# First self attention: who writes the high part of the queries, GpSimd or ScalarE

## The chip, the cores and the metric

The kernel runs on one core of a Trainium2 chip. The metric is the device time of one execution in microseconds (us); the times given are the median and the spread of several runs. A profile is one execution recorded by the hardware.

## The reference

A decoder of two layers runs over 8 sequences of 256 positions and 256 channels: attention, cross attention and a feed forward part, twice. Only the first attention matters here. It has 4 branches of 16 heads of 16 channels; all branches share keys and values. Cut to its core:

```python
q = (X @ W_Q + b_Q).reshape(Bv, Tv, H_TOT, DH).transpose(0, 2, 1, 3)
q, k = (_rope(q), _rope(k))
scores = jnp.einsum('bhtd,bhsd->bhts', q, k) * ATTNSCALE
w = jax.nn.softplus(scores / jnp.sqrt(key_self)[:, :, None, :])
w = jnp.where(causal, w, 0.0)
w = w * jax.nn.sigmoid(SCALE * w)
w = jnp.where(w < sinks, 0.0, w)
total = jnp.sum(w, axis=-1, keepdims=True) + sinks + 1e-06
out = jnp.einsum('bhts,bhsd->bhtd', w / total, v) + (sinks / total) * v_null
y = jnp.einsum('bntc,ncd->bntd', context, W_O) + W_O_bias[None, :, None, :]
```

`_rope` multiplies by a cosine and adds the other half of each pair times a sine.

## The kernel before

`attention0` writes out the order of every engine by hand. One pass of `over_batches` is a batch (a sequence) b, from -1 to 8: the work of batch b stands beside work ahead for b+1 and left over from b-1. A batch has 8 steps, one for each pair of heads; two steps are a quad of four heads. The first batch is b = 0, the second b = 1; "step 0" is the first step of a batch.

Scores: TensorE makes the scores of the next step in three slots (L386, L391), each as soon as ScalarE's softplus (L538) has emptied the slot's banks. ScalarE works slot by slot: step s, slots 0, 1, 2. In an even step it does more after slot 0: it copies the sums of an older quad out of PSUM (L525), then takes four silus (L557) over the quad before, with a table load on either side, then goes on with slot 1. In step 4 it also takes Ln and Exp for the keys (L564, L566) and copies the turned context (L515). VectorE compares each weight with its sink (L732, 16 instructions in an even step, two for each head and half) and so releases TensorE's weighted sums (L412). Between them VectorE takes other results out of two spare PSUM banks that everything else on TensorE shares in turn: the rotated queries and keys (L683), values (L691), regrouped sums (L703), the output (L722).

Queries are made a quad at a time, in even steps: the third quad of the batch in step 0, the fourth in step 2, and the first and second quad of the next batch in steps 4 and 6. Their path: TensorE projects (L435), VectorE multiplies by sine and cosine into `by_sin` and `by_cos` (L683), SP swaps neighbouring rows of `by_sin` into `turned_sin` by two DMAs (L332), GpSimd adds (`split_queries`) and splits the sum into a high part, rounded to the fp32r type, and the rest: `q_parts`. SP stores both (L337), waits, and loads them into rows (L341), all in the order of one queue, with the keys' store and loads (L349, L353) behind those of steps 4 and 6. Keys go the same way in step 2 (`square_keys`, L599 and L602) and step 4 (`split_keys`, L607 to L613). GpSimd also divides the sums of a quad (`divide`, L625 and L632). SP, GpSimd, ScalarE, VectorE and TensorE each run their own list in order and wait on semaphores. VectorE writes new rotations only when `rot_taken` says that the one before is used up.

In `split_queries` GpSimd waits for the swap, and for the rows of the previous quad to have landed (`q_here`), and then runs three 128x512 instructions: the sum into the high part (L590), the same sum into `by_cos` in full precision (L591), and the difference (L593).

Of the kernel before, what the change touches and what calls it, by code (L numbers as in the profile page):

```python
# [11 lines left out]
ALU = mybir.AluOpType  # L12
ACT = mybir.ActivationFunctionType
# [32 lines left out]
class Steps:  # L46
# [10 lines left out]
    def wait(self):  # L57

        self.eng.wait_ge(self.sem, self.base + self.n)
# [9 lines left out]
def alone(eng, sem, value, passed):  # L69

    eng.wait_ge(sem, value)
    eng.sem_inc(passed, 1)
# [22 lines left out]
def wait_alone(eng, sem, value, passed):  # L95
    if not isinstance(value, int) or value > 0:
        alone(eng, sem, value, passed)


def over_batches(eng, body):  # L100

    for b in range(-1, B + 1):
        body(b, 0 <= b < B, b + 1 < B, b >= 1)
# [97 lines left out]
PAIRS_OF_HEADS, QUADS, SLOTS = NH // 2, NH // 4, 3  # L201
# [30 lines left out]
def spare_bank(b, step, kind, i):  # L232

    return 6 + (SPARE_USES[step, (kind, i)] + b * len(SPARE_USES)) % 2
# [11 lines left out]
def quad_at(b, at, new, old):  # L246

    if at >= 0:
        return (at, b * QUADS + at) if new else None
    return (QUADS + at, b * QUADS + at) if old else None  # L250


def attention0(nc, norm, x_all, xnT_all, ident, psum, a):
    with ExitStack() as stack:
        s = Scope(nc, stack, "a0")
# [15 lines left out]
        by_cos, by_sin, turned_sin = (s.sb(n, [P, 2, T]) for n in ("by_cos", "by_sin", "turned_sin"))  # L271
        q_parts = s.sb("q_parts", [P, 2, 2, T], F32R)
# [23 lines left out]
        swapped, rot_taken, q_summed, q_split = (s.sem(n) for n in ("swapped", "rot_taken", "q_summed", "q_split"))  # L296
        ksq_ready, ln_k, knorm_ready, knormed, k_high, k_split = (
            s.sem(n) for n in ("ksq_ready", "ln_k", "knorm_ready", "knormed", "k_high", "k_split"))
        q_here, k_here = s.sems("q_here", 2), s.sems("k_here", 2)
        q_stored, k_stored = s.sem("q_stored"), s.sem("k_stored")  # L300

        scored, plus_done, silu_done, weights_done, summed, sums_taken = (
            s.sem(n) for n in ("scored", "plus_done", "silu_done", "weights_done", "summed", "sums_taken"))
# [5 lines left out]
        consts, passed, own = s.sem("consts"), s.sem("passed"), s.sem("own_setup")  # L309
# [11 lines left out]
        MOVES = 16 * PARTS  # L321
# [180 lines left out]
        @block.scalar  # L502
        def _(act):
            act.preload_act_table_set("softplus")
            act.wait_ge(consts, 1)

            def body(b, new, ahead, old):
                exists = {HERE: new, AHEAD: ahead, OLD: old}

                def take_turned(i):  # L510
                    spare = psum[:, spare_bank(b, 3 + i // 2, "turn", i), :]
                    act.wait_ge(turn_done, (b - 1) * 4 + i + 1)

                    wait(act, out_done, (b - 1) * TT + i // 2)
                    act.activation(ctxT[:, 4 * (i % 2):4 * (i % 2) + 4, :],  # L515
                                   spare.rearrange("p (k n) -> p k n", k=4), ACT.Copy).then_inc(turn_taken, 1)

                def take_sums(quad, half, bank):
                    if quad:
                        k, n = quad  # L520
                        act.wait_ge(summed, 2 * n + half + 1)
                        if half == 0:

                            wait(act, regrouped, (n - 1) * 2)
                        act.activation(sumT[:, k % 2, half * 512:(half + 1) * 512], psum[:, bank, :],  # L525
                                       ACT.Copy).then_inc(sums_taken, 1)

                def softplus(step, x):
                    pair = b * PAIRS_OF_HEADS + step
                    n = pair * SLOTS + x  # L530
                    if x == 0:

                        wait(act, summed, ((pair - PAIR_RING) // 2 + 1) * 2)
                    act.wait_ge(scored, n + 1)
                    wu = w[:, pair % PAIR_RING]
                    to, of = (wu[:, :, 2 * x:2 * x + 2, 0:T], psS[x].rearrange("p (h r t) -> p h r t", h=2, r=2)) if x < 2 else \
                        (wu[:, :, :, T:COLS], psS[x].rearrange("p (h r t) -> p h r t", h=2, r=BR))
                    act.activation(to, of, ACT.Softplus).then_inc(plus_done, 1)  # L538

                for step in range(PAIRS_OF_HEADS):  # L540
                    for x in range(SLOTS):
                        if new:
                            softplus(step, x)
                        if step % 2 == 0 and x == 0:
                            sums_quad = quad_at(b, step // 2 - 2, new, old)
                            take_sums(sums_quad, 0, spare_bank(b - (step < 1), (step - 1) % PAIRS_OF_HEADS, "sum", 0))
                            if old and step == 4:
                                take_turned(0)
                                take_turned(1)
                            quad = quad_at(b, step // 2 - 1, new, old)  # L550
                            if quad:
                                k, n = quad
                                act.wait_ge(plus_done, (n * 2 + 2) * SLOTS)
                                for pair in range(2):
                                    for h in range(2):
                                        wu = w[:, (2 * n + pair) % PAIR_RING, h].rearrange("p r t -> p (r t)")
                                        act.activation(wu, wu, ACT.Silu, scale=SILU_SCALE).then_inc(silu_done, 1)  # L557
                                        if (pair, h) == (0, 1):
                                            take_sums(sums_quad, 1, spare_bank(b, step, "sum", 1))
                            if ahead and step == 4:  # L560

                                act.preload_act_table_set("natural_log_exp_and_others")
                                act.wait_ge(norm_taken, b + 2)
                                act.activation(ksq[:], ksq[:], ACT.Ln).then_inc(ln_k, 1)  # L564
                                act.wait_ge(ln_k, b + 2)
                                act.activation(ksq[:], ksq[:], ACT.Exp, scale=-0.5, bias=ln_quarter[:, 0:1])\  # L566
                                   .then_inc(knorm_ready, 1)
                            if quad or ahead and step == 4:
                                act.preload_act_table_set("softplus")
                            if not quad:  # L570
                                take_sums(sums_quad, 1, spare_bank(b, step, "sum", 1))
                        if old and (step, x) == (5, 0):
                            take_turned(2)
                            take_turned(3)

            over_batches(act, body)

        @block.gpsimd
        def _(pool):
            pool.wait_ge(consts, 1)  # L580

            def body(b, new, ahead, old):
                exists = {HERE: new, AHEAD: ahead, OLD: old}

                def split_queries(n, r):

                    alone(pool, swapped, 32 * (r + 1), passed)

                    wait_alone(pool, q_here[(n - 1) % 2], (n - 1) // 2 * MOVES + MOVES if n > 0 else 0, passed)
                    pool.tensor_tensor(q_parts[:, 0], by_cos[:], turned_sin[:], ALU.add)  # L590
                    pool.tensor_tensor(by_cos[:], by_cos[:], turned_sin[:], ALU.add).then_inc(q_summed, 1)  # L591
                    alone(pool, q_summed, n + 1, passed)
                    pool.tensor_tensor(q_parts[:, 1], by_cos[:], q_parts[:, 0].bitcast(F32), ALU.subtract).then_inc(q_split, 1)  # L593
                    alone(pool, q_split, n + 1, rot_taken)

# [1573 lines left out]
def experts(nc, norm, x_all, xnT_all, ident, psum, a):  # L2169

    with ExitStack() as stack:
# [125 lines left out]
        def _(dve):  # L2297
# [75 lines left out]


STAGES = (("a0", attention0), ("x0", linear_attention), ("f0", switch_attention),
          ("a1", attention1), ("x1", cross_attention1), ("f1", experts))

# [120 lines left out]
```

## Time and profile before

| | |
|---|---|
| median of 3 runs | 2862.13 us (2858.52 to 2868.64) |
| the profiled execution | 2852.82 us, its span 2851.0 us |
| mean granted TensorE clock | 0.935 of full speed |
| the first attention in the span | about 28 to 720 us |
| batch b = 3 in the span | about 306 to 387 us |

The profile's busy time counts the work of an engine and not its waiting. A row of a timeline merges neighbouring instructions of one kind: start, length from the first start to the last end, engine, line, and the number behind x; in brackets stands the idle time in front of it and what ended that.

### The profile page before, as it was taken

How to read it: one execution, taken by the hardware profiler on the slowest of the kernel's cores; microseconds unless marked ns; L12 is line 12 of the kernel's file. 1: busy time of each engine (PE TensorE's matmuls, PEld its weight loads, DVE VectorE, ACT ScalarE, POOL GpSimd, SP SyncE). 2: the span in 40 equal slices, each digit the busy share in tenths (PEclk: the TensorE clock that was granted, in tenths of full speed). 3: DMA queues.
4: the chain of work that ended last, by engine and by line, in shares of the span. 5: the costliest groups of instructions: out<-in, count | busy, mean ns of one | idle time of the engine just before them, and what ended most of it. 6: DMA issues, size and time to landing. Idle time of an engine off the chain costs nothing. (4 is left out here: it accounts for less than half of the span.)

```text
span 2851.0 us, 46630 instructions
## 1 busy us (share of the span) xinstructions
PE 2412.9 (85%) x17064; PEld 1938.5 (68%) x17064; DVE 1838.9 (64%) x4048; ACT 1553.4 (54%) x3054; POOL 894.5 (31%) x889
## 2 busy tenths in 40 slices
PE   3677777776768999999799999999789999769998
PEld 2454454443555766677599889889677778558887
DVE  3788888876565566654567666667756565455544
ACT  2787888886444444445366555656555565442221
POOL 1454545442013444445311111110046565500000
PEclk7788889888888999999899999999999999979999
DMA  4333333330121111111100000000100000020000
GB/s 156 124 120 126 114 109 128 124 107 23 57 74 42 36 27 27 27 27 26 45 5 6 6 6 3 1 1 1 69 12 5 5 9 1 19 87 8 8 8 30
DMA packets 126721, 128.98 MB, mean 45 GB/s; under 512 B 59808, under 2 KB 91040, under 8 KB 125984
## 3 DMA queue, kind: packets, MB, share of 16 engines
q1 hardware_dynamic: 126496, 126.00, 13.8%
q8 instruction: 139, 2.28, 0.3%
q14 instruction: 86, 0.70, 0.1%
HBM read 79.82 MB, written 29.36 MB: 38 GB/s over the span
## 5 line engine op out<-in xcount | busy, mean ns | idle before, releaser
L732 DVE SCALAR_TENSOR_TENSOR a_w<-a_w,a_sinks 128x384 f32<-128x384 f32 x512 | 406.5, 852 | 12.1 <-ACT a_w L557 12.1
L2070 POOL TENSOR_SCALAR x_weights<-x_weights,x_sums 128x256 f32<-128x256 f32 x256 | 231.8, 924 | 272.1 <-DVE x_sums L2129 272.1
L1160 POOL TENSOR_SCALAR f_weights<-f_weights,f_sums 128x256 f32<-128x256 f32 x256 | 232.1, 924 | 267.6 <-DVE f_sums L1390 267.6
L1318 ACT ACTIVATE f_weights<-psum,f_negmax 128x256 f32<-128x256 f32 x256 | 117.7, 472 | 211.1 <-DVE f_negmax L1384 211.1
L1655 ACT ACTIVATE a_turned_w_hi<-psum 128x512 fp32r<-128x512 f32 x256 | 139.1, 596 | 142.9 <-PE psum L1565 142.8
L538 ACT ACTIVATE a_w<-psum 128x1024 f32<-128x1024 f32 x192 | 182.5, 1033 | 53.9 <-PE psum L391 53.6
L386 PE MATMUL psum<-a_q_rows,a_k_rows 64*128 64x512 f32 x384 | 106.7, 552 | 123.3 <-ACT a_w L538 99.7
L2040 ACT ACTIVATE x_weights<-x_masked_s,x_negmax 128x256 f32<-128x256 f32 x256 | 127.0, 497 | 137.2 <-DVE x_negmax L2121 137.1
L1772 DVE TENSOR_REDUCE a_negmax<-psum 128x1 f32<-128x1024 f32 x128 | 156.6, 1223 | 55.8 <-PE psum L119 51.7
L1734 POOL TENSOR_TENSOR a_xT_lo<-all_xnT_all,a_xT_hi 128x512 fp32r<-128x512 f32 x56 | 71.5, 1278 | 360.6 <-ACT a_xT_hi L1635 360.6
L557 ACT ACTIVATE a_w<-a_w 128x1536 f32<-128x1536 f32 x128 | 182.4, 1474 | 0.4
L1779 DVE TENSOR_TENSOR a_turned_w_lo<-psum,a_turned_w_hi 128x512 fp32r<-128x512 f32 x256 | 163.5, 680 | 0.2 <-ACT a_turned_w_hi L1655 0.2
L386 PEld LDWEIGHTS psum<-a_q_rows,a_k_rows 64*128 64x128 f32 x384 | 42.8, 219 | 161.0 <-ACT a_w L538 115.8
L117 PE MATMUL psum<-a_turned_w_hi,a_v_hi 128*128 128x256 f32 x512 | 150.1, 293 | 0.5 <-DVE a_turned_w_lo L1779 0.5
L1664 ACT ACTIVATE a_weights<-psum,a_negmax 128x1024 f32<-128x1024 f32 x128 | 143.4, 1120 | 2.9 <-DVE a_negmax L1772 2.8
L118 PE MATMUL psum<-a_turned_w_lo,a_v_hi 128*128 128x256 f32 x512 | 144.8, 283 | 0.0
L119 PE MATMUL psum<-a_turned_w_hi,a_v_lo 128*128 128x256 f32 x512 | 144.8, 283 | 0.0
L1565 PE MATMUL psum<-all_ident,a_weights 128*128 128x128 f32 x1024 | 132.7, 272 | 0.5 <-ACT a_weights L1664 0.5
L1565 PEld LDWEIGHTS psum<-all_ident,a_weights 128*128 128x128 f32 x1024 | 119.0, 140 | 18.2 <-ACT a_weights L1664 2.5
L412 PE MATMUL psum<-a_w,a_v 128*32 128x512 f32 (+1 forms) x1024 | 105.7, 534 | 14.7 <-DVE a_w L732 13.4
L590 POOL TENSOR_TENSOR a_q_parts<-a_by_cos,a_turned_sin 128x512 fp32r<-128x512 f32 x32 | 47.9, 1498 | 203.8 <-DMA a_turned_sin<-a_by_sin 203.8
L2367 DVE SCALAR_TENSOR_TENSOR f_acc<-psum,f_p,f_acc 128x256 f32<-128x256 f32 x112 | 54.2, 484 | 89.0 <-PE psum L119 85.6
(358 smaller groups left out, 7356.8 us busy)
## 6 DMA issues: line engine op xcount, KB each, us to landing
a_q_rows<-a_q_kept SPq DMA_DIRECT2D x128, 256.0 KB, 3.5
a_q_kept<-a_q_parts SPq DMA_DIRECT2D x32, 512.0 KB, 2.6
a_turned_sin<-a_by_sin SPq DMA_DIRECT2D x80, 128.0 KB, 2.4
a_k_rows<-a_k_kept SPq DMA_DIRECT2D x64, 128.0 KB, 3.2
a_k_kept<-a_k_parts SPq DMA_DIRECT2D x8, 512.0 KB, 5.0
f_xnT<-all_xnT_all SPq DMA_DIRECT2D x16, 256.0 KB, 2.3
f_pv_rows<-f_pv SPq DMA_DIRECT2D x8, 512.0 KB, 3.2
f_pv_groups<-f_pv_rows SPq DMA_DIRECT2D x8, 512.0 KB
```

Of the source, the lines that this page charges most:

```text
L117: pe.matmul(out, lhsT[0], rhs[0], start=start, stop=False)
L118: pe.matmul(out, lhsT[0], rhs[1], start=False, stop=False)
L119: return pe.matmul(out, lhsT[1], rhs[0], start=False, stop=stop)
L386: pe.matmul(psum[:, 2 * x + h, :], k_rows[rows[h], step, keys], queries, start=True, stop=False)
L538: act.activation(to, of, ACT.Softplus).then_inc(plus_done, 1)
L557: act.activation(wu, wu, ACT.Silu, scale=SILU_SCALE).then_inc(silu_done, 1)
L732: ins = dve.scalar_tensor_tensor(part, part, sinks[:, col:col + 1], part, ALU.is_ge, ALU.mult)
L1160: ins = pool.tensor_scalar(w, w, sums[:, k, h, t:t + 1], None, ALU.mult)
L1565: ins = pe.transpose(psum[:, 4 + half, j * P:(j + 1) * P], weights[u % 2][:, lo:lo + P], ident[:])
L1772: dve.tensor_reduce(negmax[:, u % STAT_RING:u % STAT_RING + 1], psum[:, 2 * (u % 2):2 * (u % 2) + 2, :].rearrange("p a n -> p (a n)"), AX. ...
L1779: dve.tensor_tensor(lo, psum[:, 4 + half, :].rearrange("p (j t) -> p j t", t=P), hi.bitcast(F32), ALU.subtract)\
L2070: ins = pool.tensor_scalar(w, w, sums[:, k, h, t:t + 1], None, ALU.mult)
```

## The change

ScalarE writes the high part. In an even step, after the softplus of slot 1, it waits for GpSimd's sum in `by_cos` (`q_summed`) and for the store of the previous quad to have landed (`q_stored`), and copies `by_cos` into the high part, rounded; the new semaphore `q_high` tells GpSimd, which waits for it in front of the difference. GpSimd's wait for `q_here` and its first sum are gone. For b = -1 there is no softplus, and ScalarE only does the copies of steps 4 and 6.

```diff
-        q_stored, k_stored = s.sem("q_stored"), s.sem("k_stored")
+        q_stored, k_stored, q_high = s.sem("q_stored"), s.sem("k_stored"), s.sem("q_high")
...
+                        if step % 2 == 0 and x == 1 and (new if step < 4 else ahead):
+                            n = (b + (step >= 4)) * QUADS + (step // 2 + 2) % QUADS
+                            act.wait_ge(q_summed, n + 1)
+                            wait(act, q_stored, 16 * n)
+                            act.activation(q_parts[:, 0], by_cos[:], ACT.Copy).then_inc(q_high, 1)
...
-                    wait_alone(pool, q_here[(n - 1) % 2], (n - 1) // 2 * MOVES + MOVES if n > 0 else 0, passed)
-                    pool.tensor_tensor(q_parts[:, 0], by_cos[:], turned_sin[:], ALU.add)
                     pool.tensor_tensor(by_cos[:], by_cos[:], turned_sin[:], ALU.add).then_inc(q_summed, 1)
-                    alone(pool, q_summed, n + 1, passed)
+                    alone(pool, q_high, n + 1, passed)
                     pool.tensor_tensor(q_parts[:, 1], by_cos[:], q_parts[:, 0].bitcast(F32), ALU.subtract).then_inc(q_split, 1)
```

## Rows read from the trace of the kernel before

**Rows 1.** The page, busy time: us, share of the span, instructions.
```profile
PE 2412.9 (85%) x17064; PEld 1938.5 (68%) x17064; DVE 1838.9 (64%) x4048; ACT 1553.4 (54%) x3054; POOL 894.5 (31%) x889
```
**Rows 2.** Windows, b = 3: busy us of PE, PEld, DVE, ACT, POOL; clock, DMA.
```profile
306.00:387.00 81.00, 61.58 (x404) 40.21 (x404) 66.70 (x110) 65.12 (x65) 38.93 (x35) 0.88 0.34 114
```
**Rows 3.** Groups of 28 to 720 us: busy us, mean ns, idle before and releasers.
```profile
L732 DVE SCALAR_TENSOR_TENSOR a_w<-a_w,a_sinks 128x384 f32<-128x384 f32 x512 | 406.5, 852 | 12.1 <-ACT a_w L557 12.1
...
L386 PE MATMUL psum<-a_q_rows,a_k_rows 64*128 64x512 f32 x384 | 106.7, 552 | 123.3 <-ACT a_w L538 99.7 <-DMA a_k_rows<-a_k_kept 17.5 <-DMA a_q_rows<-a_q_kept 5.7
...
L590 POOL TENSOR_TENSOR a_q_parts<-a_by_cos,a_turned_sin 128x512 fp32r<-128x512 f32 x32 | 47.9, 1498 | 203.8 <-DMA a_turned_sin<-a_by_sin 203.8
```
**Rows 4.** Timeline, GpSimd and VectorE: thresholds beside GpSimd, then two without.
```profile
305.97 1.59 POOL L590 TENSOR_TENSOR a_q_parts<-a_by_cos,a_turned_sin 128x512 fp32r<-128x512 f32 x1 [6.63 <-DMA a_turned_sin<-a_by_sin]
...
309.29 1.37 POOL L593 TENSOR_TENSOR a_q_parts<-a_by_cos,a_q_parts 128x512 fp32r<-128x512 f32 x1 [0.18 <-POOL a_by_cos L591]
...
306.36 4.72 DVE L732 SCALAR_TENSOR_TENSOR a_w<-a_w,a_sinks 128x384 f32<-128x384 f32 x3
...
318.23 1.14 DVE L732 SCALAR_TENSOR_TENSOR a_w<-a_w,a_sinks 128x384 f32<-128x384 f32 x2
```
**Rows 5.** Groups, shapes apart, ScalarE: a copy from SBUF in the second layer.
```profile
L1635 ACT ACTIVATE a_xT_hi<-all_xnT_all 128x512 fp32r<-128x512 f32 x56 | 34.9, 623 | 0.0
```
**Rows 6.** Timeline, step 0 of b = 3, then of b = 1.
```profile
306.03 4.69 ACT L538 ACTIVATE a_w<-psum 128x1024 f32<-128x1024 f32 x5
...
308.13 0.69 PE L386 MATMUL psum<-a_q_rows,a_k_rows 64*128 64x512 f32 x2
...
316.65 0.48 DVE L683 SCALAR_TENSOR_TENSOR a_by_sin<-psum,a_bq,a_rope 128x256 f32<-128x256 f32 x1 [1.08 <-PE psum L435]
...
149.06 1.94 ACT L538 ACTIVATE a_w<-psum 128x1024 f32<-128x1024 f32 x2
...
149.36 3.02 POOL L590 TENSOR_TENSOR a_q_parts<-a_by_cos,a_turned_sin 128x512 fp32r<-128x512 f32 x1 [7.45 <-DMA a_turned_sin<-a_by_sin]
```
**Rows 7.** Timeline, step 2 of b = 3: VectorE, then SP's queue.
```profile
323.48 6.00 DVE L732 SCALAR_TENSOR_TENSOR a_w<-a_w,a_sinks 128x384 f32<-128x384 f32 x8
...
332.10 0.47 DVE L683 SCALAR_TENSOR_TENSOR a_by_sin<-psum,a_bk,a_rope 128x256 f32<-128x256 f32 x1
...
330.48 2.58 SPq L341 DMA_DIRECT2D a_q_rows<-a_q_kept  x4
333.77 1.15 SPq L332 DMA_DIRECT2D a_turned_sin<-a_by_sin  x2
```
**Rows 8.** Timeline, step 4 of b = 3; last, waits of 61 to 720 us.
```profile
346.99 2.86 ACT L538 ACTIVATE a_w<-psum 128x1024 f32<-128x1024 f32 x3
...
343.96 1.36 POOL L590 TENSOR_TENSOR a_q_parts<-a_by_cos,a_turned_sin 128x512 fp32r<-128x512 f32 x1 [3.30 <-DMA a_turned_sin<-a_by_sin]
...
343.59 6.80 DVE L732 SCALAR_TENSOR_TENSOR a_w<-a_w,a_sinks 128x384 f32<-128x384 f32 x5
...
PE psum L461 <- DVE a_ctx L703: 7.4, 5, 2.7
```
**Rows 9.** Timeline, TensorE, the meeting point behind step 6 of b = 3.
```profile
380.46 1.50 PE L412 MATMUL psum<-a_w,a_v 128*32 128x512 f32 x16 [0.39 <-DVE a_w L732]
```
**Rows 10.** Timeline, first batch: ScalarE, GpSimd, VectorE, SP.
```profile
61.47 3.86 ACT L538 ACTIVATE a_w<-psum 128x1024 f32<-128x1024 f32 x4 [17.84 <-PE psum L391]
...
75.05 1.02 ACT L538 ACTIVATE a_w<-psum 128x1024 f32<-128x1024 f32 x1 [5.59 <-PE psum L391]
...
76.66 1.28 POOL L590 TENSOR_TENSOR a_q_parts<-a_by_cos,a_turned_sin 128x512 fp32r<-128x512 f32 x1 [11.50 <-DMA a_turned_sin<-a_by_sin]
...
80.78 0.48 DVE L683 SCALAR_TENSOR_TENSOR a_by_sin<-psum,a_bq,a_rope 128x256 f32<-128x256 f32 x1 [12.26 <-POOLq L72]
...
73.05 1.24 SPq L332 DMA_DIRECT2D a_turned_sin<-a_by_sin  x2
...
85.91 1.24 SPq L332 DMA_DIRECT2D a_turned_sin<-a_by_sin  x2
```

## The prediction

> **What bounds the kernel now.** The page's busy times come first [rows 1]: no engine is full over the span, so the share says little about one stage. The chain of waits of the page covers only the last stage, so I read the first attention from its windows, its groups and its timelines. The whole change lies between 28 and 720 us. In a middle batch of 81.0 us [rows 2] VectorE is busy 66.7, ScalarE 65.1 and TensorE 61.6 us; none fills it. The batch is a ring. TensorE's scores wait 99.7 us in the stage for ScalarE's softplus, and only once, 5.7 us, for queries to arrive from DRAM [rows 3]. So queries that are ready earlier are worth nothing by themselves. Two chains run side by side from one even step to the next: ScalarE to TensorE (softplus, scores, sums, projection) and VectorE (16 thresholds, L732, then the copies that free a PSUM bank). Whichever comes last at a meeting point sets the time, and the margin there is 0.3 to 2.7 us. So each of the four even steps of a batch has to be summed for itself.
>
> The second thing to see is a lock. Behind a GpSimd sum, three thresholds follow each other in 4.72 us, 1.6 us apart; two with no GpSimd work beside them take 1.14 us, 0.53 us apart after the first's 0.61 [rows 4]. So a 128x512 GpSimd sum costs VectorE about 1.07 us if VectorE is then in thresholds.
>
> **What the change adds and removes.** 32 GpSimd sums into the high part (L590) go: 47.9 us of GpSimd, 1498 ns each [rows 3]. GpSimd is no end of either chain: it waits 203.8 us in front of these sums for the swapped halves [rows 3]. What they give back is therefore VectorE's 1.07 us each, where VectorE is last. 32 ScalarE copies of 128x512 from SBUF come in. The trace has this very shape and type: 623 ns [rows 5]. Neighbouring activations start 0.92 us apart at 1.02 us each [rows 6], 0.10 us inside each other, so a copy takes 0.52 us of ScalarE's queue. No table load comes with it: the trace's copies into the sums (L525) stand between softplus and silu without one of their own.
>
> The copy also adds a wait. ScalarE's queue is in order; behind the copy stand the softplus of slot 2, the next step's three, and the silus, so TensorE waits for all of them. In the other direction GpSimd's subtraction waits for the copy, and behind it stand the key split (step 4) and the division; the store of the queries on SP waits too.
>
> **Step 0 (third quad's queries).** In the batch shown, the softplus of slot 1 ends at 307.05, and the first sum would end at 305.97 + 1.59 = 307.56 [rows 4, 6]: 0.51 wait + 0.52. TensorE takes that slot's successor at 308.13 with no gap and runs on to the projection, for which VectorE has already waited 1.08 us [rows 6]. So this cost is bare, and VectorE's saving is hidden. The second batch is worst: its sum ends at 152.38, its slot 1 at 150.09 [rows 6], a wait of 2.29. In the other five a sum ends before the softplus. Seven batches: 7 x 0.52 + 2.29 + 0.51 = **+6.4 us** (3.6 if the second batch's 3.02 us sum is a chance).
>
> **Step 2.** Here VectorE is last: eight thresholds take 6.00 us beside two GpSimd operations, and the key rotation follows without a gap at 332.10 [rows 7]. With one operation fewer up to 1.07 us goes. But SP's swap at 333.77 comes only 0.71 us behind the end of the query loads (330.48 + 2.58) [rows 7], and these do not come earlier, since the subtraction starts 0.1 us later than before. I take 0.6 of 1.07, the share that SP leaves: 7 x 0.6 = **-4.2 us** (0 to -7.5).
>
> **Step 4.** ScalarE is late here: slot 1 ends at 348.01, while the sum would be ready at 345.32 [rows 8]. GpSimd stands for some 3 us, its key split starts 1.7 us later, and in this pause VectorE's thresholds run unhindered: the five from 343.59 took 6.80 us, and ended 350.4 [rows 8]. Three of them leave the lock, so VectorE gains up to 3 us. But TensorE's transposes (L461) wait for VectorE only 7.4 us in five batches, 2.72 at most [rows 8]; when that is used up, the copy's 0.52 shows on TensorE's own side. So -7.4 + 6 x 0.52 (the second batch has no such wait) = -4.3, and -1.2 in the first batch, whose VectorE chain keeps about one lock's worth: **-5.5 us** (+3 if nothing comes back, -8 if all does).
>
> **Step 6.** VectorE saves about 1 us, but at the next meeting point TensorE waits for it only 0.39 us [rows 9], and TensorE's chain is 0.52 late. So 0.52 - 0.39, about +0.15, in the four batches that run like this one, and the full 0.52 in the three others with this step, where I reckon with no such margin: **+2.1 us** (-3 to +4).
>
> **The first batch.** The copy for the third quad sits behind the second softplus of all, which ended at 63.4; its sum ended only at 76.66 + 1.28 = 77.94 [rows 10]. ScalarE, in order, stands 14.5 us. Six softplus then come at once, and the one that began at 75.05 [rows 10] begins at about 78.9 + 4 x 0.95 = 82.7, 7.7 us late. Cover: the start is paced by SP, whose swaps follow one after the other (73.05, 85.91) [rows 10]. The rotation behind that softplus began at 80.78 and lasted four instructions, to about 82.4 [rows 10]; 7 us later it ends near 89.4, so SP's swap slips from 85.91 to 89.5, 3.6 us, of which the shorter query split returns about 0.6. I take **+3 us** (0 if SP covers all, 7.7 if nothing).
>
> **Sum.** 6.4 - 4.2 - 5.5 + 2.1 + 3 = +1.8 us. The profiled execution took 2852.8 us, span 2851.0; that becomes about 2855. The median of the runs, 2862.1, lies 9.3 above it, so the time is **2864 us**. Ends: 3.6 - 7.5 - 8 - 3 + 0 = -15 and 6.4 + 0 + 3 + 4 + 7.7 = +21; the terms don't all fall to one side, so the likeliest case's own range is -7 to +8.5.
>
> **The rivals.** *Faster: the lock's relief reaches the end.* If VectorE's chain leads at each of the 28 meeting points behind the start, 28 x 1.07 = 30 us come back, less 28 x 0.52 = 15 for the copies in front of it: -15, 2847 us. For it: the lock is the plainest thing in the rows [rows 4]. Against: at steps 0 and 6 VectorE already waits or has 0.39 us in hand [rows 6, 9]. The Trainium skill's page "SBUF — State Buffer" (section "Who interferes with whom") says that VectorE and GpSimd share a port pair under an exclusive lock and that ScalarE never waits on anyone. By that alone each sum moved to ScalarE is a clear gain, -30 us here (2832). The trace agrees on the lock (0.53 against 1.6 us apart) but shows ScalarE's queue as a link of the chain, which that rule leaves out.
>
> *Slower: ScalarE's queue takes the lead.* Every copy and wait is bare, and VectorE's saving only makes it wait longer: 28 copies x 0.52 = 15, the waits of 2.8 in step 0 [rows 6], 3 to 7.7 at the start: +21 to +25, 2883 to 2887. It decides once ScalarE's side is over 0.7 us behind VectorE's at steps 2 and 4. For it: 99.7 us of scores waiting for softplus [rows 3], and the second batch already goes that way in step 4. Against: the key rotation in step 2 follows VectorE alone [rows 7], and the turn's transposes wait for VectorE in five batches [rows 8]. A half of it (steps 2 gains nothing, the start costs 7) gives +11, 2873.
>
> *It doesn't do what it says:* GpSimd's freed 1.5 us go into waiting for the copy, and the pause doesn't help VectorE, since its threshold then meets the later key split instead. That leaves step 4 at +3 and step 2 at 0: +15, 2877; it joins the slower side.
>
> **How the numbers follow.** A difference under 0.3% (8.6 us) can't be told from none here. Forecast (within 2853.5 to 2870.7) 0.60; ScalarE's lead, whole or half, 0.20 and the missing relief 0.07, together slower 0.27; relief that reaches the end, faster 0.13. The range of 8 in 10 takes in the half case and the edge of the faster one: 2851 to 2878. The likeliest case alone: 2855 to 2871.
>
> **What would show it.** In the changed kernel: a ScalarE copy of 0.62 us 32 times; ScalarE's idle in front of it about 14.5 us once, 2.3 once, under 1 elsewhere; thresholds 0.53 apart in the pause between GpSimd's sum and its subtraction; the waits of the turn's transposes for VectorE down from 7.4 to under 3 us; softplus starts after the step 0 copy 0.5 to 1 us later against the batch's own start; the period of the batch shown near 80 us. A first batch that is over 6 us longer, or step 2 that does not shorten, would make the prediction too low; a period under 79 too high. A copy of over 0.8 us, or a table load beside it, would break the basis.

## The result, and the profile after

The changed kernel took 2871.71 us (median of 7 runs, 2863.54 to 2882.66); the kernel before, beside it on the same chip, took 2858.52 (7 runs, 2853.5 to 2868.64). The ratio is 1.0046, with a 95% interval of 1.0029 to 1.0064: slower by 13 us. That is inside the range I gave, but not my likeliest case, a difference that can't be told from none. The time lies between that case (up to 2870.7) and the half of the "ScalarE's queue takes the lead" rival (2873); as a difference, +13 is a little above that half's +11.

The profiled execution after has a span of 2869.9 us, 18.9 longer than before. The first attention is 16.1 of that; the rest comes behind it, where the code is the same. First its busy times, as in [rows 1]:

```profile
PE 2419.3 (84%) x17064; PEld 1946.2 (68%) x17064; DVE 1801.2 (63%) x4048; ACT 1573.6 (55%) x3086; POOL 846.8 (30%) x857
```

GpSimd lost 47.7 us of work and VectorE 37.7, ScalarE took on 20.2, and the time went up. The groups of the stage show where that went (columns as in [rows 3]):

```profile
L735 DVE SCALAR_TENSOR_TENSOR a_w<-a_w,a_sinks 128x384 f32<-128x384 f32 x512 | 366.6, 776 | 11.7 <-ACT a_w L557 11.7
L386 PE MATMUL psum<-a_q_rows,a_k_rows 64*128 64x512 f32 x384 | 111.1, 575 | 160.3 <-ACT a_w L538 142.6 <-DMA a_k_rows<-a_k_kept 17.7
L594 POOL TENSOR_TENSOR a_by_cos<-a_by_cos,a_turned_sin 128x512 f32<-128x512 f32 x32 | 49.4, 1545 | 212.3 <-DMA a_turned_sin<-a_by_sin 212.3
L596 POOL TENSOR_TENSOR a_q_parts<-a_by_cos,a_q_parts 128x512 fp32r<-128x512 f32 x32 | 43.3, 1354 | 68.0 <-ACT a_q_parts L576 68.0
L576 ACT ACTIVATE a_q_parts<-a_by_cos 128x512 fp32r<-128x512 f32 x32 | 20.1, 627 | 46.1 <-POOL a_by_cos L594 46.1
```

VectorE's thresholds did get 40 us shorter (852 to 776 ns each), so the lock's relief is real. The copy costs what [rows 5] say, 627 ns. But ScalarE stands 46.1 us in front of its copies, and TensorE's scores wait 142.6 us for softplus instead of 99.7 [rows 3]. The waits of 61 to 725 us (who, for whom; total, times, longest) complete it:

```profile
ACT a_q_parts L576 <- POOL a_by_cos L594: 46.1, 10, 19.2
PE psum L461 <- DVE a_ctx L706: 0.7, 1, 0.7
```

The transposes' wait for VectorE, 7.4 us in [rows 8], is used up, as forecast.

To see which step paid, I took the starts of slot 1's softplus (L538) in the even steps from both traces, and summed each stretch from one even step to the next over the batches. All later traces are measured in the same way. The column "0" is the seven stretches from step 0 to step 2, and so on; "start" reaches to step 4 of the first batch. One trace each, in us against the kernel before:

```
          start    0      2      4      6    end   stage
after      +3.2  +12.2   -2.8  -11.8  +14.7  +0.7  +16.1
s24        +0.7   -0.5   +1.8  -12.5   +3.5  +3.7   -3.3
s06        +1.3  +14.2   -0.3   -5.7   +1.2  +0.0  +10.7
relief     -6.1   +2.7   -7.0   -9.1   -4.3  +2.2  -21.6
copy       +2.2   +8.3   -0.1   -4.5   +3.8  +2.0  +11.8
late       +0.7   +8.8   -4.4  -14.8  +14.1  +3.5   +8.0
early4     +2.3  +12.8   -1.0  -16.9   +7.3  +2.1   +6.6
spkeys     -2.8  +12.1   -2.4  -12.5   +3.9  +4.8   +3.1
best       +1.3  +14.1   +2.2  -16.8   -1.1  +3.5   +3.2
sporder    -1.2   +0.6    0.0   -6.6   +0.1  +0.9   -6.2
s24sp      -3.0   +0.1   +0.2  -12.9   -2.0  +0.7  -16.9
s246sp     -4.7   +1.2   +0.2   -9.5   +2.5  +2.1   -8.2
```

Steps 0 and 6 lost 27 us, step 4 won 12. The rest of the time behind the stage differs by -1.5 to +11.4 us from trace to trace with the same code there, so verdicts go by the medians, and the table only says where. Even there a column can be off by some 6 us: s06 leaves step 4 as it was before, and shows -5.7 in it.

**Step 0.** The timeline of b = 2 (start, length, engine, line; in brackets the idle time in front and its releaser):

```profile
233.35 1.02 ACT L538 ACTIVATE a_w<-psum 128x1024 f32<-128x1024 f32 x1
236.68 0.63 ACT L576 ACTIVATE a_q_parts<-a_by_cos 128x512 fp32r<-128x512 f32 x1 [2.31 <-POOL a_by_cos L594]
...
232.51 4.14 POOL L594 TENSOR_TENSOR a_by_cos<-a_by_cos,a_turned_sin 128x512 f32<-128x512 f32 x1 [5.97 <-DMA a_turned_sin<-a_by_sin]
...
231.21 4.32 DVE L735 SCALAR_TENSOR_TENSOR a_w<-a_w,a_sinks 128x384 f32<-128x384 f32 x8
...
238.28 0.80 PE L386 MATMUL psum<-a_q_rows,a_k_rows 64*128 64x512 f32 x2 [2.63 <-ACT a_w L538]
```

The sum took 4.14 us. VectorE's eight thresholds ran through at 0.54 us each meanwhile: here VectorE kept the lock and GpSimd starved, the reverse of [rows 4]. ScalarE stood 2.31 us for that sum and TensorE 2.63 behind ScalarE. Windows of the 10 us that follow this softplus, first of the kernel before (b = 2, 5), then of the changed one (columns as in [rows 2]):

```profile
226.10:236.10 10.00, 8.88 (x60) 6.13 (x61) 9.67 (x14) 7.60 (x9) 6.92 (x8) 0.66 0.36 125
464.00:474.00 10.00, 8.92 (x64) 6.11 (x64) 9.47 (x12) 8.60 (x9) 7.98 (x8) 0.83 0.25 93
```
```profile
233.30:243.30 10.00, 6.24 (x38) 4.11 (x41) 4.67 (x11) 6.38 (x8) 6.26 (x4) 0.56 0.18 67
475.70:485.70 10.00, 6.28 (x40) 4.16 (x44) 4.67 (x11) 6.34 (x7) 6.22 (x4) 0.57 0.18 62
```

In b = 2 TensorE gets 38 matmuls done instead of 60, at a granted clock of 0.56 instead of 0.66: more of the stretch runs at the lower of its two levels (1.2 GHz instead of 2.4). In b = 1 and 4, where ScalarE did not stand, the clock over the same 10 us was as low (0.54 in both, against 0.74 and 0.67 before), the group of 16 (L412) in this step took 2.64 and 2.60 us instead of 1.50 and 1.55, and the step still cost 2.2 and 1.6.

**Step 4.** The timeline of b = 3, to be set beside [rows 8], and one row of the kernel before at the same place:

```profile
359.61 0.63 ACT L576 ACTIVATE a_q_parts<-a_by_cos 128x512 fp32r<-128x512 f32 x1
...
354.24 1.34 POOL L594 TENSOR_TENSOR a_by_cos<-a_by_cos,a_turned_sin 128x512 f32<-128x512 f32 x1 [3.21 <-DMA a_turned_sin<-a_by_sin]
360.42 1.27 POOL L596 TENSOR_TENSOR a_q_parts<-a_by_cos,a_q_parts 128x512 fp32r<-128x512 f32 x1 [4.84 <-ACT a_q_parts L576]
...
367.37 1.50 PE L412 MATMUL psum<-a_w,a_v 128*32 128x512 f32 x16
```
```profile
358.01 2.79 PE L412 MATMUL psum<-a_w,a_v 128*32 128x512 f32 x16
```

GpSimd's pause is there: 4.84 us, not 3. TensorE's group of 16 took 1.50 us instead of 2.79. The kernel before has such a slow group in step 4 of b = 2, 3, 5 and 6 (2.57, 2.79, 2.53, 2.79), and just these four batches got shorter, by 3.1, 4.4, 1.8 and 3.8 us; the other three changed by 0 to +0.9. The group's own part is 4.7 us of it.

**Step 6.** The timeline of b = 3, changed kernel, then before:

```profile
373.13 2.53 SPq L353 DMA_DIRECT2D a_k_rows<-a_k_kept  x4
375.70 1.24 SPq L332 DMA_DIRECT2D a_turned_sin<-a_by_sin  x2
...
373.25 0.48 DVE L686 SCALAR_TENSOR_TENSOR a_by_cos<-psum,a_bq,a_rope 128x256 f32<-128x256 f32 x1
...
378.25 1.03 ACT L538 ACTIVATE a_w<-psum 128x1024 f32<-128x1024 f32 x1
380.19 0.63 ACT L576 ACTIVATE a_q_parts<-a_by_cos 128x512 fp32r<-128x512 f32 x1 [0.92 <-POOL a_by_cos L594]
...
383.02 1.12 PE L454 MATMUL psum<-all_ident,a_sumT 128*128 128x128 f32 x4
```
```profile
359.33 2.53 SPq L353 DMA_DIRECT2D a_k_rows<-a_k_kept  x4
366.50 1.15 SPq L332 DMA_DIRECT2D a_turned_sin<-a_by_sin  x2
...
370.92 3.77 ACT L538 ACTIVATE a_w<-psum 128x1024 f32<-128x1024 f32 x4
...
373.69 0.66 PE L454 MATMUL psum<-all_ident,a_sumT 128*128 128x128 f32 x4
```

Before, the key loads left SP 11.6 us ahead of step 6's softplus, and the swap 4.4 ahead. After, the loads are only 5.1 us ahead. Counted from slot 1 of step 4 (346.99 before [rows 8], 358.69 after) they leave 2.1 us later, since the key split stood behind the copy; the other 4.4 us of their lead are gone because step 4 itself had become that much shorter. The swap, whose rotation was done at 373.73, must follow them on SP at 375.70. So its sum is late, ScalarE stands 0.92 us, and the matmuls behind run slower (1.12 against 0.66). This wait is 2.32 us in b = 2 and 2.84 in b = 6. By batches step 6 lost 5.1, 2.7 and 4.1 us in b = 2, 3 and 6, those in which step 4 had won most, and 2.8 in the other four together. So step 6 gives back in these three batches what step 4 had won there (11.9 against 11.3 us); steps 4 and 6 together come to +2.9, and what is left as a net loss in this trace is step 0.

**The first batch.** The timeline of ScalarE and SP, beside [rows 10]:

```profile
64.26 0.63 ACT L576 ACTIVATE a_q_parts<-a_by_cos 128x512 fp32r<-128x512 f32 x1 [19.20 <-POOL a_by_cos L594]
80.74 0.63 ACT L576 ACTIVATE a_q_parts<-a_by_cos 128x512 fp32r<-128x512 f32 x1 [14.02 <-POOL a_by_cos L594]
...
91.57 0.51 SPq L332 DMA_DIRECT2D a_turned_sin<-a_by_sin  x1
```

These two waits make up 33.2 of the 46.1 us, and the start came out only 3.2 us longer.

### The profile page after: what moved, and what is told of

It is laid out like the page before. It is cut to its first block and busy times, and to the rows that moved or that the text cites. A ratio compares the mean times of both kernels' runs of the same rounds, so it can differ in the third digit from the quotient of the medians.

```text
span 2869.9 us, 46631 instructions
## 1 busy us (share of the span) xinstructions
PE 2419.3 (84%) x17064; PEld 1946.2 (68%) x17064; DVE 1801.2 (63%) x4048; ACT 1573.6 (55%) x3086; POOL 846.8 (30%) x857
## 5 line engine op out<-in xcount | busy, mean ns | idle before, releaser
L735 DVE SCALAR_TENSOR_TENSOR a_w<-a_w,a_sinks 128x384 f32<-128x384 f32 x512 | 366.6, 776 | 11.7 <-ACT a_w L557 11.7
L386 PE MATMUL psum<-a_q_rows,a_k_rows 64*128 64x512 f32 x384 | 111.1, 575 | 160.3 <-ACT a_w L538 142.6
L538 ACT ACTIVATE a_w<-psum 128x1024 f32<-128x1024 f32 x192 | 185.2, 1028 | 34.8 <-PE psum L391 34.4
L594 POOL TENSOR_TENSOR a_by_cos<-a_by_cos,a_turned_sin 128x512 f32<-128x512 f32 x32 | 49.4, 1545 | 212.3 <-DMA a_turned_sin<-a_by_sin 212.3
L412 PE MATMUL psum<-a_w,a_v 128*32 128x512 f32 (+1 forms) x1024 | 102.5, 521 | 10.4 <-DVE a_w L735 10.2
L117 PE MATMUL psum<-a_kT_hi,a_qT_hi 128*128 128x512 f32 x256 | 103.5, 404 | 8.5 <-issue 6.9
```

What stands on the lines that cost most here:

```text
L117: pe.matmul(out, lhsT[0], rhs[0], start=start, stop=False)
L386: pe.matmul(psum[:, 2 * x + h, :], k_rows[rows[h], step, keys], queries, start=True, stop=False)
L735: ins = dve.scalar_tensor_tensor(part, part, sinks[:, col:col + 1], part, ALU.is_ge, ALU.mult)
```

## The experiments

Three theories. A: the loss is where ScalarE's queue leads, in steps 0 and 6 (wait, copy, and TensorE's clock behind the stop). B: GpSimd's pause in step 4 makes keys and SP late, and step 6 pays. C: each copy's 0.52 us of queue is bare wherever it stands. Each ratio is against the kernel before on the same chip.

**Half of the copies.** In s24 ScalarE copies in steps 2 and 4 alone, in s06 in steps 0 and 6 alone; the other halves stay with GpSimd. (This diff and those that follow are cut, with constants written out.)

```diff
-                        if step % 2 == 0 and x == 1 and (new if step < 4 else ahead):
+                        if step in (2, 4) and x == 1 and (new if step < 4 else ahead):
...
+                    if n % 4 in (2, 1):
+                        wait_alone(pool, q_here[(n - 1) % 2], ...)
+                        pool.tensor_tensor(q_parts[:, 0], by_cos[:], turned_sin[:], ALU.add).then_inc(q_high, 1)
```

(s06: `step in (0, 6)` and `n % 4 in (3, 0)`.)

> ScalarE writes the high part only in steps 2 and 4; in steps 0 and 6 GpSimd makes three operations as before. Theory A (the loss sits where ScalarE's queue leads, steps 0 and 6: wait, copy, and TensorE's clock behind the idle): the gain of steps 2 and 4 stays, 8 to 15 us faster than before. Theory B (GpSimd's pause in step 4 makes the keys and SP late, and step 6 pays for it): step 6 still loses, within 5 us of before. Theory C (each copy costs its 0.52 us wherever it stands): 16 copies, 6 to 8 us slower.

> ScalarE writes the high part only in steps 0 and 6. Theory A: 18 to 28 us slower than before, more than the whole change, since nothing is given back. Theory B: step 6 has no late keys, so about 10 us slower, less than the whole change. Theory C: 16 copies, 6 to 8 us slower.

s24: 2856.03 us, ratio 0.9993 [0.9978, 1.0008]. s06: 2874.74, 1.0061 [1.0039, 1.0084]. The whole loss is in steps 0 and 6. C falls as the one cause: with the same number of copies, s06 loses 17 us, twice the 6 to 8 that C gave it. (s24 alone would not show this, as the 16 sums that it takes off VectorE's way could hide a cost of that size.) The waits in front of the copies, s24 then s06 (28 to 725 us):

```profile
ACT a_q_parts L577 <- POOL a_by_cos L598: 8.1, 2, 7.1
```
```profile
ACT a_q_parts L577 <- POOL a_by_cos L598: 39.9, 5, 18.5
```

Of these, 7.1 and 32.9 us are in the first batch. Behind it s06 has three waits of 2.3 us, all in step 0 (b = 3, 5, 7), and these batches lose most there (3.1, 3.8, 3.0).

Against A, s24 was not faster, though its step 4 won 12.5 us in the trace; and s06 lost its time in step 0 (+14.2), while step 6 lost 1.2. So step 6's loss needs the copy in step 4 as well, as B says. By the median, though, s06's +17 is nearer to A's 18 to 28 than to B's 10, and not less than the whole change's +13: step 0 alone is enough for the net loss.

**Each half of the edit by itself.** relief drops the copy and has GpSimd sum straight into the high part; the low part is then made from a `by_cos` that holds only the cosine product, so that sum is left out.

```diff
-                    pool.tensor_tensor(q_parts[:, 0], by_cos[:], turned_sin[:], ALU.add)
-                    pool.tensor_tensor(by_cos[:], by_cos[:], turned_sin[:], ALU.add).then_inc(q_summed, 1)
+                    pool.tensor_tensor(q_parts[:, 0], by_cos[:], turned_sin[:], ALU.add).then_inc(q_summed, 1)
```

> GpSimd makes two operations, no copy on ScalarE, no pause: the sum goes straight into the high part, and the low part is taken from the cosine product alone, so the full sum is left out and the low parts are wrong. It prices VectorE's relief from the lock alone. Theory A: VectorE leads in steps 2 and 4, so 8 to 15 us faster than before. Theory C: GpSimd is on no chain, and without copies nothing moves, within 3 us.

2837.74 us, 0.9939 [0.9921, 0.9956]: 17.5 us won, more than the 8 to 15 expected. So about half of 32 x 1.07 = 34 us of lock reaches the end. The copy kernel is the kernel before with a copy of the same size from a table at the same places and no new hand-off:

```diff
+                        if step % 2 == 0 and x == 1 and (new if step < 4 else ahead):
+                            n = (b + (step >= 4)) * QUADS + (step // 2 + 2) % QUADS
+                            wait(act, copied_once, n)
+                            act.activation(spare_high[:], rope[:], ACT.Copy).then_inc(copied_once, 1)
```

> The kernel before with a ScalarE copy of the same size in the same places, of a constant table into a scratch tile, that waits for nothing new; GpSimd as before. It prices the copy's own time in ScalarE's queue. Theory A: steps 2 and 4 have room, steps 0 and 6 pay, 5 to 10 us slower. Theory C: 30 copies bare, about 15 us slower, the whole loss.

2864.81 us, 1.0030 [1.0018, 1.0042]: +8.6, as A had it and not C's 15; the trace puts +8.3 into step 0. The queue's 0.52 us is bare there (7 x 0.52 = 3.6, the rest comes with slower matmuls) and covered in step 2. If the parts add up, -17.5 + 8.6 = -9 would be the change without its hand-off; it measured +13, so by subtraction the waits between ScalarE and GpSimd, and what they make late, cost some 22 us; no run measures this by itself. Most of the 8.3 sits in b = 3, 6 and 7 (1.8, 2.3, 1.9), where the group of 16 took 2.27, 2.63 and 2.63 us. The 10 us from slot 1 of step 0 in b = 6, before and in the copy kernel (columns as in [rows 2]):

```profile
541.80:551.80 10.00, 8.93 (x63) 6.27 (x64) 9.46 (x13) 8.31 (x9) 7.45 (x8) 0.75 0.30 101
```
```profile
548.67:558.67 10.00, 8.71 (x50) 5.05 (x52) 9.58 (x14) 6.58 (x8) 6.92 (x8) 0.54 0.38 135
```

**Where the copy stands.** late puts it one slot later in all four steps; early4 moves only step 4's copy, to right behind Exp, in front of the softplus's table load.

```diff
-                        if step % 2 == 0 and x == 1 and (new if step < 4 else ahead):
+                        if step % 2 == 0 and x == 2 and (new if step < 4 else ahead):
```

> The change with ScalarE's copy behind the softplus of slot 2 in place of slot 1; nothing else. Theory A (in steps 0 and 6 ScalarE waits for the sum, and TensorE's scores stand behind it): by one softplus later the sum is there and TensorE has the slot it needs next, so step 0's loss goes, 8 to 14 us faster than the change, about as fast as before. Theory C (the copy's 0.52 us bare wherever it stands): as slow as the change, within 4 us.

2867.49 us, 1.0038 [1.0025, 1.0050]. A's cure fails: step 0 keeps +8.8. But the wait is not gone. In b = 1, 4, 6 and 7 the copy still stands 1.4 us for a slow sum, and just these four lose 2.2 to 2.9 us, each with a group of 16 at 2.79 us; b = 2, 3 and 5, without a wait, change by -0.9 to +0.1. So A's mechanism stands and its cure was too short. The timeline of b = 1:

```profile
150.40 3.94 POOL L594 TENSOR_TENSOR a_by_cos<-a_by_cos,a_turned_sin 128x512 f32<-128x512 f32 x1 [8.79 <-DMA a_turned_sin<-a_by_sin]
...
154.37 0.63 ACT L576 ACTIVATE a_q_parts<-a_by_cos 128x512 fp32r<-128x512 f32 x1 [1.42 <-POOL a_by_cos L594]
...
158.06 2.79 PE L412 MATMUL psum<-a_w,a_v 128*32 128x512 f32 x16
```

```diff
+                                n = (b + 1) * QUADS
+                                act.wait_ge(q_summed, n + 1)
+                                wait(act, q_stored, 16 * n)
+                                act.activation(q_parts[:, 0], by_cos[:], ACT.Copy).then_inc(q_high, 1)
...
+                        if step in (0, 2, 6) and x == 1 and (new if step < 4 else ahead):
```

> The change with step 4's copy moved up, behind Exp and in front of the table load; steps 0, 2, 6 as in the change. GpSimd's pause of 2 to 5 us in step 4 nearly goes and the keys are early. Theory B (late keys hold up SP, so step 6's sum is late): the loss between steps 6 and 0 falls from 14.7 to under 5 us, but the gain between steps 4 and 6 shrinks too; in all 3 to 8 us faster than the change. If the pause was what helped VectorE and the keys do not matter: no better than the change, or slower.

2861.64 us, 1.0016 [1.0004, 1.0027], 0.3% under the change, within the 3 to 8 us of B or just above. In the trace step 6's loss falls to 7.3, not under 5, and step 4 does not gain less, as B had it, but 5 us more: B's side, with its account of step 4 wrong.

**SP's order.** spkeys is the change with the first half of the key loads behind step 6's swap instead of in front of it (the keys' store stays in step 4); sporder is that order on the kernel before.

```diff
+                        if step == 6:
+                            place_keys(b + 1, 0)
...
-                        if step >= 4:
-                            place_keys(b + 1, i)
+                        if step == 4:
+                            sp.wait_ge(k_split, b + 2)
+                            sp.dma_start(k_kept, k_parts[:].bitcast(F32)).then_inc(k_stored, 16)
+                        if step == 6:
+                            place_keys(b + 1, 1)
```

> The change with SP's order alone altered: the loads of the keys' first rows (step 4) stand behind the swap of step 6; the store of the keys stays where it was. Theory B: GpSimd's sum in step 6 is no longer late, ScalarE's waits there (0.4 to 2.8 us, five times) go, 5 to 9 us faster than the change. If SP's queue is not the cause: no difference beyond 3 us.

> The kernel before with SP's new order alone (loads of the keys' first rows behind the swap of step 6); ScalarE and GpSimd as before. Theory B says that order matters because the change makes the keys late: without the change the keys' loads end 4.6 us ahead of the swap in the batch shown, so within 4 us of before. Rival: the order is a gain by itself and would have made up for anything: 8 to 14 us faster than before, and then it says nothing on the change.

spkeys: 2858.36 us, 1.0001 [0.9986, 1.0015]: the change's loss is gone, 13 us where I had expected 5 to 9, and step 6 takes +3.9 instead of +14.7. Its timeline, step 6 of b = 3: the swap leaves ahead of the loads, and the copy has no wait.

```profile
359.77 1.36 SPq L332 DMA_DIRECT2D a_turned_sin<-a_by_sin  x2
361.25 2.60 SPq L351 DMA_DIRECT2D a_k_rows<-a_k_kept  x4
...
365.18 0.62 ACT L579 ACTIVATE a_q_parts<-a_by_cos 128x512 fp32r<-128x512 f32 x1
```

sporder: 2848.57 us, 0.9972 [0.9953, 0.9991]; I had expected no more than 4 us of it. It is the low end of what the rival said, that the order is a gain by itself. So the order is worth 8 us without the change, and of the 13 in spkeys only some 5 are left for its interplay with the copy, which the intervals don't tell from none. For the interplay speak the traces: the swap that stood behind the loads, and step 6 without its waits. Where the order's own 8 us come from isn't shown: sporder's trace has -6.6 in step 4, but s06, with step 4 as before, has -5.7.

**Versions built from these.** best: copies one slot later in steps 0, 2 and 6, early in step 4; the third and fourth quad of the first batch stay with GpSimd.

```diff
+                        if (step in (0, 2) and x == 2 and new and b > 0) or (step == 6 and x == 2 and ahead):
```

> Copies behind slot 2 in steps 0, 2 and 6, in front of the table load in step 4, and the third and fourth quad of the first batch by GpSimd as before. Theories A and B together: waits gone, VectorE's relief kept (17 us without any copy), so 6 to 14 us faster than before. Theory C: no faster than before.

2865.38 us, 1.0019 [1.0008, 1.0030]: missed. ScalarE stands in front of the copy in step 0 of all seven batches, 10 us in sum, and step 0 loses 14.1. Its timeline there, b = 5:

```profile
465.81 2.54 POOL L602 TENSOR_TENSOR a_by_cos<-a_by_cos,a_turned_sin 128x512 f32<-128x512 f32 x1 [8.19 <-DMA a_turned_sin<-a_by_sin]
...
468.38 0.63 ACT L581 ACTIVATE a_q_parts<-a_by_cos 128x512 fp32r<-128x512 f32 x1 [1.41 <-POOL a_by_cos L602]
...
472.08 2.31 PE L413 MATMUL psum<-a_w,a_v 128*32 128x512 f32 x16
```

Even one slot later the starved sum (2.54 us) is not ready, and TensorE's group of 16 takes 2.31 us; over the seven batches it took 2.25 to 2.79. Last, SP's order with copies in steps 2 and 4 (s24sp), and in 2, 4 and 6 (s246sp):

```diff
+                        if step == 6:
+                            place_keys(b + 1, 0)
...
-                        if step % 2 == 0 and x == 1 and (new if step < 4 else ahead):
+                        if step in (2, 4) and x == 1 and (new if step < 4 else ahead):
...
+                    if n % 4 in (2, 1):
+                        pool.tensor_tensor(q_parts[:, 0], by_cos[:], turned_sin[:], ALU.add).then_inc(q_high, 1)
```

(s246sp: `step in (2, 4, 6)` and `n % 4 in (2,)`.)

> ScalarE's copy in steps 2 and 4 only, with SP's new order. Theories A and B: nothing waits in steps 0 and 6 any more, and SP is not held up by the keys, so the gain of step 4 (12 us between steps 4 and 6 with the old order) is kept in part: 5 to 12 us faster than before. If the gain was never VectorE's: as before, within 4 us.

> ScalarE's copy in steps 2, 4 and 6, with SP's new order; only step 0 stays with GpSimd. Theory A: what is left of the loss in the run with the whole change and the new order sits in step 0 (12 us), so this is 8 to 14 us faster than before. If step 6's copy costs as much as step 0's: within 4 us of before.

s24sp: **2840.31 us, 0.9932 [0.9908, 0.9956]**, the fastest that leaves nothing out, 0.7% under the kernel before. s246sp: 2844.80, 0.9956 [0.9939, 0.9973]. s24sp won more than the 5 to 12 us expected, s246sp what A gave it. Step 6's copy is no gain even with SP's order. Beside sporder in the same series s24sp is 8 us faster, while s24 was not told from the kernel before: with SP out of the way, the copies in steps 2 and 4 pay. That this is step 4's win no longer given back fits the trace (step 6 -2.0 instead of +3.5), but s24sp's lead over s24 beyond the order's 0.28% is about as large as the intervals.

## Why the prediction was right or wrong

**Right in kind, and in size with luck.** The chain runs through ScalarE's queue, the lock's relief reaches the end only in part, and no table load came. The range held because it reached to the half of the slower rival: the sum of the terms, +1.8 us, was 11 short, and in the trace step 6 (12.6 too low) and step 4 (6.3 too high) were off against each other. That each sum moved is a clear gain, which I drew from "SBUF — State Buffer" in the Trainium skill ("Who interferes with whom"), came out with the wrong sign. The lock is there, but relief alone won 17.5 us, not 30. ScalarE waited 46.1 us here, on a semaphore, which the rule that it never waits on anyone, one of ports, leaves out; 33.2 of them are in the first batch, and the two of 2.31 in step 0 are for sums of 4.14 and 3.62 us.

**First batch:** +3 forecast, +3.2 in the trace. SP's swap slipped to 91.57, against 89.5 forecast; one further wait, 19.20 us in front of the very first copy, was not in my sum. So the agreement is partly luck.

**Step 0, the first term that failed in size:** +6.4 forecast, +12.2 measured, and +14.2 in s06. I took the second batch's 3.02 us sum for the worst of seven. The starved sum turns up in other batches (b = 2 and 5, each with a wait of 2.31 us), so waits are 4.6 us instead of 2.8. The larger miss is the copy itself. In the four kernels with the copy behind slot 1 in step 0 (the change, s06, early4, spkeys) the 11 batches with a wait lost 2.5 to 3.8 us there, 3.2 on average, and the 17 without one 0.3 to 2.2, 1.0 on average. So a wait counts at about its own length, and the copy at 1.0 us where I had 0.52. In the copy kernel step 0 takes 8.3 us instead of 3.6, and its three dear batches ran at a granted clock of 0.54 to 0.57 over 10 us, against 0.71 to 0.75 before.

**Step 2:** -4.2 forecast, -2.8 measured.

**Step 4:** -5.5 forecast, -11.8 measured. The pause is there and the 7.4 us are used up, as described. What I missed is that four batches ran there with slow matmuls. In b = 3 every kernel gains (1.8 to 5.2 us) and in b = 5 every one but copy (1.5 to 2.5), s06 with an untouched step 4 too, so that part is not the change's doing. In b = 2 and 6 the gain (2.8 to 4.9 us each) comes with ScalarE's copy of the high part in step 4, in every kernel that has it (but for late in b = 6), and is at most 0.9 in copy, s06, relief and sporder. It does not go by the length of the pause: early4 and best, with pauses of 0.8 to 2.1 us in these two batches, gain 3.6 to 4.8. That the pause frees VectorE is therefore not shown to be its cause.

**Step 6, the step that failed:** "0.52 - 0.39, about +0.15, in the four batches that run like this one, and the full 0.52 in the three others", +2.1 in all and +4 at most; it was +14.7. I had named the chain in the second paragraph on the change (the key split waits behind the subtraction), and then summed step 6 as if its sum stayed early. I did not follow the key loads into SP's in-order queue, where step 6's swap stands behind them, nor see that a shorter step 4 brings step 6's copy closer to them. In the traces, copy in step 4 alone (+3.5), in step 6 without step 4 (+1.2), and the other order of SP (+3.9) each take most of the loss away.

**What would have shown it:** I said that idle of 14.5 us once, 2.3 once and under 1 elsewhere would be right. Two waits of 2.3 us in step 0 and two of 2.3 and 2.8 in step 6 are the failure. The period of b = 3, "near 80 us", came out at 79.4, 1.2 shorter than before. This batch, from which most rows were read, is the only one of b = 1 to 6 that got shorter, so no sign read from it alone could show the loss.

**The rivals.** Half of "ScalarE's queue takes the lead" (+11) comes closest in size, by its lead in steps 0 and 6 and not by step 2, for which it had no gain. Open: how the 13 us of spkeys divide between the order's own gain and the interplay; why step 4 runs slowly in some batches of the kernel before and not in others; and by what way the copy in step 4 ends that.

## What to carry to other kernels

A copy moved to another engine is paid in that engine's queue and in the two hand-offs: here -17.5 for the lock, +8.6 for the queue and, by subtraction, some +22 for waiting. The place decides: the queue's part showed in step 0 and was covered in step 2, and s24 lost nothing where s06 lost 17 us. Place it only where the producer is early and nothing on the consumer's way (a DMA queue included) becomes late; here that was two places of four, and they paid only with SP's new order. Follow every step that stands behind a delayed instruction through SP's queue up to the next meeting point before costing that point.

## What the runs showed of the hardware

- With VectorE and GpSimd both at work, either can be the one held up: in [rows 4] thresholds went 1.6 us apart beside a 1.59 us sum; in step 0 of b = 2 eight went at 0.54 us while one sum took 4.14.
- Where TensorE had stood for ScalarE in step 0, more of the time behind ran at the lower clock: granted clock 0.56 and 0.57 over 10 us, against 0.66 and 0.83 in the kernel before; in late and best the groups of 16 behind such a stop took 2.25 to 2.79 us instead of 1.50. A copy of 0.52 us without a wait could do it too: 0.54 to 0.57 in three batches of the copy kernel, against 0.71 to 0.75.
- The order of DMA issues on SP alone moved the time by 0.28% [0.09, 0.47], with the same transfers.
